# New orders around a dense tile, and one product of each tile moved from VectorE to ScalarE and GpSimd

## What is computed

```
q, k = rope(bf16(x @ Wq.T)), rope(bf16(x @ Wk.T))            # one head of 256
o    = sum over k <= q of exp(q.k / 16)                      # one number per row
x1   = layernorm(x + relu(o @ fc1_w.T + fc1_b) @ fc2_w.T + fc2_b)

xa   = x1 @ P_w.T                                            # 64 columns
Ci   = softmax over the top 3 of xa @ Ui.T, i = 1, 2, 3      # weights over 12 experts
h    = gelu(sum_e C1[:, e] * (x1 @ W1[e].T))                 # first mixture
y    = sum_e C2[:, e] * (h @ W2[e].T) + C3 @ b2              # second mixture, bias
out  = layernorm(x1 + y)
```

## Time and profile before

| | |
|---|---|
| median of 3 runs | 302.46 us (302.26 to 304.33) |
| profiled execution, its own time | 302.41 us |
| its span, first to last instruction | 300.5 us |
| busy in the span | PE 268.8 us (89%), DVE 239.7 (80%), ACT 164.0 (55%), POOL 148.8 (50%) |
| mean granted TensorE clock | 0.979 of full speed |

### The profile page before, as it was taken

The page is one execution under the profiler, slowest core; times in us unless marked ns, Lnnn a source line. Parts: engine busy times, 40 slices in busy tenths (PEclk is TensorE's granted clock), DMA queues, the critical chain, the costliest instruction groups (busy, mean ns, idle before and its releaser), DMA issues.

```text
span 300.5 us, 6389 instructions
## 1 busy us (share of the span) xinstructions
PE 268.8 (89%) x2028; PEld 195.1 (65%) x2030; DVE 239.7 (80%) x696; ACT 164.0 (55%) x341; POOL 148.8 (50%) x317
## 2 busy tenths in 40 slices
PE   6997999999896947999989989999999999999980
PEld 4443445544354724897877877877778788788960
DVE  0377689789708986689999999999999989987871
ACT  1246846663771645056656656846837847446430
POOL 2200008999998964242571572482373372573421
PEclk9999999999999995799999999999999999999998
DMA  8998999970000000000010001001000101011011
GB/s 229 403 397 279 164 193 205 150 100 0 0 3 0 0 3 0 0 12 29 17 27 28 22 17 37 20 19 38 19 20 22 34 20 35 21 35 30 27 35 40
DMA packets 19483, 20.50 MB, mean 68 GB/s; under 512 B 1636, under 2 KB 18808, under 8 KB 18936
## 3 DMA queue, kind: packets, MB, share of 16 engines
q1 hardware_dynamic: 18456, 19.13, 26.9%
q10 hardware_dynamic: 992, 0.93, 1.1%
HBM read 15.83 MB, written 4.19 MB: 67 GB/s over the span
## 4 chain that ended last, share of the span: by engine, by line
PE 39%; DVE 27%; POOL 15%; issue 7%; SPq 4%; DMA 4%; ACT 2%; DVEq 0%; POOLq 0%
PE bank L942 31%; DVE early L1309 10%; POOL W L417 5%; DMA W<-in_w2T 4%; POOL wtmp L414 4%; POOL W L416 3%; PE bank L780 2%; DVE early L1366 2%; SPq L341 2%; PE bank L828 2%; DVE st L1361 2%; DVE top L1177 2%; DVE x1T L1167 1%; DVE zrest L1192 1%; DVE xturn L1085 1%
## 5 line engine op out<-in xcount | busy, mean ns | idle before, releaser
L942 PE MATMUL bank<-W,early 128*128 (+1 forms) x630 | 76.9, 279 | 5.4 <-DVE early L1366 5.4
L942 PE MATMUL bank<-W,x1T 128*128 (+1 forms) x630 | 75.0, 273 | 2.3 <-ACT early L684 1.2
L942 PEld LDWEIGHTS bank<-W,early 128*128 128x128 f16 x630 | 61.0, 100 | 17.8 <-DVE early L1366 7.1
L942 PEld LDWEIGHTS bank<-W,x1T 128*128 128x128 f16 x630 | 59.8, 98 | 13.2 <-issue 2.9
L1309 DVE SCALAR_TENSOR_TENSOR early<-bank,Csel,early 128x256 f32<-128x256 f32 x124 | 59.8, 482 | 7.8 <-PE bank L942 3.2
L780 PE MATMUL bank<-early,wqk 128*128 128x512 f32 x128 | 60.3, 602 | 3.4 <-ACT qk L568 2.2
L1085 DVE TENSOR_TENSOR xturn<-qk,turn 128x2048 bf16<-128x2048 bf16 x16 | 21.4, 1335 | 21.1 <-ACT qk L568 21.0
L525 POOL TENSOR_SCALAR ve<-mv 128x1 f32<-128x1 f32 x32 | 7.3, 229 | 61.6 <-DVE mv L1362 60.8
L780 PEld LDWEIGHTS bank<-early,wqk 128*128 128x128 f32 x128 | 22.3, 190 | 23.8 <-issue 20.8
L689 ACT ACTIVATE early<-early 128x256 f32<-128x256 f32 x32 | 13.3, 417 | 44.8 <-DVE early L1309 44.6
L568 ACT ACTIVATE qk<-bank 128x512 bf16<-128x512 f32 x32 | 18.9, 594 | 28.8 <-PE bank L780 28.6
(11 more groups left out here) (116 smaller groups left out, 434.1 us busy)
## 6 DMA issues: line engine op xcount, KB each, us to landing
early<-in_xT SPq DMA_DIRECT2D x16, 256.0 KB, 7.2
xs<-in_x SPq DMA_DIRECT2D x32, 128.0 KB, 7.5
out<-early SPq DMA_DIRECT2D x32, 128.0 KB
W<-in_w1T SPq DMA_DIRECT2D x1, 2048.0 KB, 11.8
W<-in_w2T SPq DMA_DIRECT2D x1, 2048.0 KB, 12.4
W<-in_w1T SPq DMA_DIRECT2D x1, 1024.0 KB, 7.2
W<-in_w2T SPq DMA_DIRECT2D x1, 1024.0 KB, 14.0
wqk<-in_wqkT ACTq DMA_DIRECT2D x1, 512.0 KB, 3.8
```

The costliest lines, as they stand in the source:

```text
L942: mm = pe.matmul(where[:, 0:DIM], lhs(hx, c), w, start=(k == 0), stop=(k == 5))
```

## The change

Four things are changed.

1. **Bound of the second mixture's weights.** `w_sum` works in six halves rather than three pieces, and all six stand in chunks 2 and 3 rather than 1 and 2. `w_bound` and `peak_transpose` stand later in chunk 3.
2. **Orders between the chunk loop and turn 4.** Turns 1 to 3 are no longer turns of the loop: each engine has a list of its own. Tile 0's transposition and six of its second products stand right behind the first mixture of tile 1, in the order of experts 4 to 11, then 0 to 3 (`dense_expert`). The statistics of group 3 (`norm_stats(3)`) stand at the end of VectorE's list, `normed(3, 0)` near the end of ScalarE's, and the last `w_piece` ahead of `norm_scale(2)`.
3. **Tiles 2 to 30 (`late`).** The second mixture's first product is scaled by ScalarE into a buffer `part` (`begin_second`), VectorE adds the two others onto x1, and GpSimd adds `part` last (`late_add`).
4. **The rows' statistics, scale and final rows of those tiles come one turn later**: `row_stats`, `row_scale` and `final` of tile i-3 in turn i. In the last turn both tile 30 and tile 31 have theirs.

```
+        def late(t):
+            return 2 <= t < NT - 1
...
-                act = key[1] == 0 and key[2] == 0
+                act = key[2] == 0 and (key[1] == 0 or late(key[0]))
...
+        def dense_expert(m, j):
+            return (j + NB * m) % NE
...                                                        GpSimd
-            norm_scale(2)
             w_piece(piece)
+            norm_scale(2)
+            def late_add(t):
+                pool.wait_ge(acc_begun, taker[slot[t, 1, 0]][1])
+                pool.wait_ge(slot_added, by_dve[last(t, 1)])
+                pool.tensor_tensor(y[:, t % 4, :], y[:, t % 4, :], part[:, t % 2, :], ALU.add).then_inc(late_added, 1)
+            bias_add(0, 0)
+            bias_add(0, 1)
+            row_scale(0)
+            chosen_exps(1)
+            weights_of(1)
+            C3_split(1)
+            select_of(1)
+            row_scale(1)
+            norm_scale(3)
+            for i in range(GT, NT + 2):
                 aux(k, s, 0)
+                if late(i - 2):
+                    late_add(i - 2)
+                if late(i - 3):
+                    row_scale(i - 3)
+                if not late(i - 2):
+                    row_scale(i - 2)
                 aux(k, s, 1)
...                                                        ScalarE
-                act.activation(junk[:, :, :], Wf[:, WS:2 * WS, :][:, PARTS[q], :], ACT.Abs,
+                act.activation(junk[:, 2 * r:2 * r + 2, :], Wf[:, WS:2 * WS, :][:, HALVES[q], :], ACT.Abs,
...
+            def begin_second(t):
+                n = slot[t, 1, 0]
+                wait(act, late_added, t - 3)
+                act.wait_ge(slot_done, n + 1)
+                act.activation(part[:, t % 2, :], bank[place[n]][:, 0:DIM], ACT.Copy, scale=Csel[:, t, 1, 0:1])\
+                    .then_inc(acc_begun, 1)
...
+            h_high(2)
+            C3T_copy(1)
+            begin(3)
+            gelu(3)
+            normed(3, 0)
+            final(1)
+            for i in range(GT, NT + 2):
                 aux(k, s, 0)
+                if late(i - 2):
+                    begin_second(i - 2)
                 if i <= NT:
+                    h_high(i - 1)
                 aux(k, s, 1)
+                if i < NT:
                     begin(i)
                     gelu(i)
+                if late(i - 3):
+                    final(i - 3)
+                if not late(i - 2):
+                    final(i - 2)
...                                                        TensorE
             C3_transpose(0)
+            pe.wait_ge(exp_done, SPC * NCH)
+            h_transpose(0)
+            bias(0, 0)
+            routed_first(1)
+            route_logits(1)
+            pe.wait_ge(w_split, NM * (NE - NB) - 2)
+            second(0, range(0, 6))
             gate_transpose(NCH - 1)
+            bias(0, 1)
+            x1_transpose(2, 0)
+            pe.wait_ge(w_split, NM * (NE - NB))
+            second(0, range(6, NE - NB))
+            pe.wait_ge(wlo_done, NM * NB)
+            second(0, range(NE - NB, NE))
             pe.wait_ge(hgT_copied, NCH)
+            h_transpose(1)
+            routed_first(2)
+            route_count(1)
+            x1_transpose(2, 1)
+            fc(3, 0)
+            second(1, range(TOPK))
+            h_transpose(2)
+            fc(3, 1)
+            C3_transpose(1)
+            routed_first(3)
...                                                        VectorE
+            first_mixture(0, range(8, NE))
             norm_stats(2)
+            h_low(0)
+            first_mixture(1)
+            second_mixture(0, range(0, 3))
             w_low(NB + 2)
+            route_max(1)
+            second_mixture(0, range(3, 6))
             w_low(NB + 3)
+            second_mixture(0, (6, 7))
+            route_strike(1)
+            second_mixture(0, range(8, NE))
+            row_stats(0)
+            h_low(1)
+            x1_low(2, 0)
+            route_mask(1)
+            first_mixture(2)
+            route_sums(1)
+            fc_add(3, 0)
+            route_ids(1)
+            second_mixture(1)
+            row_stats(1)
+            x1_low(2, 1)
+            h_low(2)
+            fc_add(3, 1)
+            first_mixture(3)
+            norm_stats(3)
+            for i in range(GT, NT + 2):
                 aux(k, s, 0)
+                second_mixture(i - 2)
+                if late(i - 3):
+                    row_stats(i - 3)
+                if not late(i - 2):
+                    row_stats(i - 2)
+                if i <= NT:
+                    h_low(i - 1)
                 aux(k, s, 1)
+                if i < NT:
                     first_mixture(i)
```

More of the change, by code:

```diff
@@ L322, in build @@
         PARTS = (slice(0, NB), slice(NB + 2, NB + 6), slice(NB + 6, WS))
+        HALVES = [slice(p.start + 2 * n, p.start + 2 * n + 2) for p in PARTS for n in range(2)]
         block = ctx.enter_context(nc.Block())
@@ L692, in _ @@
                 qk_copy(c, 0)
+                if c == 3:
+                    w_sum(4)
                 qk_copy(c, 1)
@@ L711, in _, with h_high, final @@
                 early_aux(c, 3, early)
-                if c in (1, 2):
-                    w_sum(2 * (c - 1))
+                if c == 2:
+                    w_sum(2)
+                    w_sum(3)
                 if c in (4, 5):
                     w_high(2 * (c - 4) + 1)
+            def h_high(t):
+                act.wait_ge(hT_done, t + 1)
+                act.activation(hT[:, t % 2, 0, :, :].rearrange("p c n -> p (c n)"), bank[HT][:, 0:DIM], ACT.Copy,
+                               scale=ipow2[:, 1:2]).then_inc(hhi_done, 1)
+            def begin_second(t):
[4 more added lines that the diff above has]
+                    .then_inc(acc_begun, 1)
+            def final(t):
+                p = t % 2
+                act.wait_ge(rstd2_done, t + 1)
+                act.activation(y[:, t % 4, :], y[:, t % 4, :], ACT.Identity, bias=shift2[:, p:p + 1],
+                               scale=rstd2[:, p:p + 1]).then_inc(y_done, 1)
             x1_high(1, 1)
@@ L1011, in _, with h_transpose @@
             first(range(8, NE))
-            C3_transpose(0)
-            gate_transpose(NCH - 1)
-            aux(0, 0, 0)
-            load_ids(0)
-            mixture(1, 0, lambda hx, c: x1T[:, 1, hx, c, :], range(TOPK))
-            aux(0, 0, 1)
-            pe.wait_ge(exp_done, SPC * NCH)
-            pe.wait_ge(hgT_copied, NCH)
-            for i in range(1, NT + 2):
+            def h_transpose(t):
+                pe.wait_ge(gelu_done, t + 1)
+                wait(pe, hlo_done, t)
+                for c in range(NC):
+                    tr = pe.transpose(bank[HT][:, c * P:(c + 1) * P], hact[:, t % 2, c * P:(c + 1) * P], identf[:, :])
+                tr.then_inc(hT_done, 1)
@@ L1031, in _ @@
-                if i <= NT:
-                    t = i - 1
-                    pe.wait_ge(gelu_done, t + 1)
-                    wait(pe, hlo_done, t)
-                    for c in range(NC):
-                        tr = pe.transpose(bank[HT][:, c * P:(c + 1) * P], hact[:, t % 2, c * P:(c + 1) * P], identf[:, :])
-                    tr.then_inc(hT_done, 1)
-                aux(k, s, 1)
-                if 1 < i < NT:
-                    t = i
-                    if t % GT == 0:
-                        load_ids(t // GT)
-                    mixture(t, 0, lambda hx, c: x1T[:, t, hx, c, :], range(experts_of(t)))
+                second(i - 2, range(TOPK))
@@ L1323, in first_mixture, with second_mixture, row_stats, h_low @@
                     add_slot(t, 0, j, sums, sums)
+            def second_mixture(t, js=range(TOPK)):
+                sums = y[:, t % 4, :]
+                for j in js:
+                    if j == 0 and late(t):
+                        continue
+                    if j == (1 if late(t) else 0):
+                        dve.wait_ge(bias_added, t // 2 + 1)
+                        wait(dve, stored[t % 4], 16 * (t // 4))
+                        add_slot(t, 1, j, sums, xs[:, t, :])
+                    else:
+                        dve.wait_ge(slot_added, by_dve[t, 1, j] - 1)
+                        add_slot(t, 1, j, sums, sums)
+            def row_stats(t):
+                p = t % 2
+                dve.wait_ge(slot_added, by_dve[last(t, 1)])
+                if late(t):
+                    dve.wait_ge(late_added, t - 1)
+                wait(dve, rstd2_done, t - 1)
+                link(dve.bn_stats(st2[:, p, :], y[:, t % 4, :]))
+                dve.bn_aggr(mv2[:, p, :], st2[:, p, :]).then_inc(mv2_done, 1)
+            def h_low(t):
+                dve.wait_ge(hhi_done, t + 1)
+                dve.scalar_tensor_tensor(hT[:, t % 2, 1, :, :].rearrange("p c n -> p (c n)"), bank[HT][:, 0:DIM],
+                                         ipow2[:, 1:2], hT[:, t % 2, 0, :, :].rearrange("p c n -> p (c n)"),
+                                         ALU.mult, ALU.subtract).then_inc(hlo_done, 1)
             route_ids(0)
```

138 lines of the change are left out of this document (61 added, 77 removed).

## The result

The changed kernel takes 305.69 us (median of 20 runs, 303.47 to 308.64), the kernel before 302.28 (20 runs, 300.57 to 304.46): a ratio of 1.0096, 95% interval 1.0073 to 1.0119. The ratio is taken over the executions of both kernels, not from the two medians, whose quotient is 1.0113, and it leaves out the changed kernel's longest execution, which counts as slow. I had forecast 303.2 us, "within 1%" as the likeliest class, and 297.0 to 306.5 as the range; the median is inside it, 2.5 us above the point, and 0.2 us outside the case's own range of 300.5 to 305.5. The profiled execution took 304.10 us (span 302.3), 1.6 us less than the median.

What follows compares the result with a forecast made beforehand. VectorE and TensorE were taken as both near their bound in steady groups, with GpSimd nearly on the path; -0.6 - 0.8 + 2.5 - 1.6 + 1.25 = +0.75 on 302.41 gave 303.2 us, range 297.0 to 306.5.

Steps and rivals of the forecast that it cites:

- the case: The forecast itself: 303.2 us for the whole kernel, own range 300.5 to 305.5, chance 0.46.
- Step 3: Groups 1 to 4: GpSimd's late adds delay `bias_add` and `normed`, TensorE stops; 4 x 0.62 = +2.5 us.
- Step 4: Groups 5 to 7: no `normed` behind `bias_add`, so TensorE's waits for VectorE's low half go; -1.6 us.
- Step 1: Weights' bound in the chunk loop: the 2.22 us stall goes, a 1.7 us wait replaces 0.89; -0.6 us.
- Step 2: Dense stretch before turn 4: routing 1.8 us earlier, but `begin(4)` hardly moves; -0.8 us.
- Step 5: The end: tile 30's statistics and row steps stand ahead of tile 31's, delaying the last final row; +1.25 us.
- A: Rival: VectorE's relief pays in every one of groups 1 to 4, -1.1 us each; 296.3 us, chance 0.25.
- B: Rival: the dense stretch pays in full, 300.5 us, or 299 if TensorE keeps the high clock; chance 0.11.
- C: Rival: GpSimd's late adds and VectorE block each other in groups' turns 1 and 2; 307.8 us, chance 0.15.

Runs made afterwards that it cites:

- run 3: The changed kernel with `begin_second` ahead of `normed` on ScalarE in each group's fourth turn: 303.71 us, ratio 1.0032 to the kernel before.
- run 9: run 3 with GpSimd's second bias addition moved into its idle gap in the group's second turn: 302.55 us, ratio 0.9985 to the kernel before.
- run 12: run 10 with ScalarE's `normed(k + 3, 0)` moved into its gap between begin and gelu of the fourth turn: 291.39 us, ratio 0.9627.
- run 8: The changed kernel with run 7's orders, run 5's, new orders entering the groups, row scaling ahead of the late add, tile 30 not handed over: 298.76 us, ratio 0.9837.
- run 6: The changed kernel with GpSimd's `bias_add(k, 1)` at the start of the group's third turn, ahead of late add and row steps: 311.32 us, ratio 1.0263.
- run 7: The changed kernel with the orders of run 3 and run 6 together: 307.18 us, ratio 1.0118 to the kernel before.
- run 5: The changed kernel with VectorE's `w_bound` ahead of the first query rotation in the fourth chunk: 305.63 us, ratio 1.0066 to the kernel before.
- run 2: The kernel before with the hand-over of tiles 2 to 30 and later row statistics alone, without the new orders: 305.44 us, ratio 1.0095.
- run 10: run 8 with the bias addition in GpSimd's second-turn gap and the third turn's `norm_scale` behind its late add: 296.79 us, ratio 0.9798.
- run 11: The changed kernel with no tile handed over, run 5's order and new orders entering the groups: 299.55 us, ratio 0.9889 to the kernel before.

## Why the prediction was right, and where it was not

**Step 3, groups 1 to 4: right in mechanism, slightly large in size.** I had written `normed` later by 0.65 to 0.75, TensorE stopped "some 2 us" and periods of 24.0. Measured from the group's first route step, `normed` starts 0.68 later (20.25 us behind it, where it was 19.57); TensorE stops 1.92, and the periods are 23.85, 0.47 longer in place of 0.62. One sign did not come as written: `normed` waits for `bias_add` in four places, but 0.7 us and not over 1. The late add that no row had shown took 721 to 730 ns, where I had taken 0.7. One wait I had not seen: `final` for the row steps, 1.15 us, which stands ahead of the other. And one gain I had not counted: VectorE's cast in `route_ids` took 0.93 us in these groups before, and 0.19 us after, since `bias_add` no longer runs beside it (see step 4). Runs 3, 9 and 12 show the cycle by taking it apart, link by link. One stated bound was wrong: I called a period of 22.2 us the most that a faster VectorE can give. Run 12 reaches 21.8, all but 0.1 us of it TensorE's own work.

**Step 4, groups 5 to 7: the step that failed.** I wrote "There is no `normed` behind `bias_add` any more, so the relief counts", and -1.6 us. Measured: +0.35 in group 5, -0.74 in groups 6 and 7, -0.4 together. TensorE's waits for the low half in the steady turns did go, 1.6 us; in their place it waits 1.4 us for `begin_second`, in two places, and 0.57 for VectorE's L1264. The first, in the changed kernel:

```profile
242.08 0.72 POOL L535 TENSOR_TENSOR early<-early 128x256 f32<-128x256 f32 x1
...
243.86 0.27 POOL L543 TENSOR_SCALAR shift<-mv,rstd 128x1 f32<-128x1 f32 x1
...
244.16 0.60 ACT L775 ACTIVATE early<-early,shift,rstd 128x256 f32<-128x256 f32 x1 [1.20 <-POOL shift L543]
...
244.66 0.45 ACT L769 ACTIVATE early<-bank,Csel 128x256 f32<-128x256 f32 x1
...
245.17 1.49 PE L1018 MATMUL bank<-W,x1T 128*128 x12 [0.63 <-ACT early L769]
```

I had asked who stands behind `normed`, and not who stands behind `final`, though the change put a 0.7 us add ahead of the row steps for which `final` waits, and put a new instruction behind `final`. Run 8 turned the two around on GpSimd, among other edits; this stop is gone there, and group 5 went to 19.77.

The second is a collision that I had not looked for. VectorE's cast of 8 numbers in `route_ids` (L1314) ends 0.02 to 0.03 us after `bias_add` whenever it starts beside it, in all fourteen profiles:

```profile
247.38 1.27 POOL L447 TENSOR_TENSOR xs<-early,x 128x512 f32<-128x512 f32 x1
...
247.75 0.93 DVE L1314 CAST ids<-idf 1x8 int32<-1x8 f32 x1
248.60 0.67 DVE L1264 TENSOR_TENSOR x1T<-bank,x1T 128x512 f16<-128x512 f32 x1
...
249.41 0.39 PE L954 MATMUL bank<-cb,C 128*72 128x128 bf16 x4 [0.57 <-DVE x1T L1264]
```

It took 0.93 us here, 0.51 in the kernel before, and 0.18 in runs 6 and 7, where `bias_add` is done by then: there TensorE's 0.57 us are gone and group 5 takes 20.24, with the first stop still in place. So the later `bias_add` does cost in group 5, though no `normed` stands behind it.

**Step 1, the weights' bound: the wait was foreseen, its price was not.** Forecast: a wait of 1.7 us and -0.6 us net. Measured in the profile: 2.02 us, since x landed at 37.8 where I had 37.1, and -0.2. I treated a stop of TensorE as costing its own length. Of the seven traces with this stop, six have the clock down behind it, and the second route step 1.5 to 4 us later. That this is most of the median's excess over the profile is inferred from those profiles and the executions' mean clocks. Run 5, which took the stop away, recovered only 0.3%, with overlapping intervals; another stop and another stretch at 0.50 had come at 77 us.

**Step 2, the dense stretch: the total about right, by two errors that cancel.** Turn 4's route step came 3.4 us earlier (I had 1.8), `begin(4)` at 140.49 in place of 142.0. But TensorE idled 1.55 and 0.95 us there, and its granted clock was 0.54 in the next 3 us; with the hand-over's own 0.5 the first period took 3.2 us. The stretch at 0.50 that the kernel before had from 113.5 to 123.8 us is gone. At turn 8 the sum is -0.2; by steps 1, 2 and one group of step 3 I had -0.8.

**Step 5, the end: right.** +1.25 forecast, +1.19 measured, and gone when tile 30 was not handed over.

**The sum.** -0.2 at turn 8, which has a group's cost in it, then 1.4 for three more groups, 0.35, -0.74 and 1.19: +2.0 at the last row's start, and +1.69 in the profiled times, where I had +0.75. At the last row's start that is 1.27 too much: 0.6 from the time up to turn 8, -0.45 from three groups that cost less than forecast, 1.2 from step 4. The other 1.6 us between the point and the median are in no term of the sum: it was made for one profiled execution. That the median still lies in the range, by 0.8 us, and the ratio within 1%, by 0.04%, is in part luck.

**Rivals.** A fell because the relief is spent in the cycle; run 12 shows that it was there to be had, with periods below A's 22.3. B got its early turn 4 and lost it at once. C's price did not come: no late add took over 0.73 us, VectorE's adds kept to 0.42 to 0.49, and the mask instruction (L1301) took 0.75 us at the median and 1.30 at most, where it had a median of 1.11. But that GpSimd and VectorE hold each other up is seen, in the mask and in the cast of step 4; it was the old `bias_add` that did it, at its new times, and not the late add. For an addition of two inputs the Trainium skill, in "GPSIMD Engine Reference", section "Engine selection", says that GpSimd is about two times slower; here 725 ns against VectorE's 483 ns for 256 columns is 1.5, with one of VectorE's operands in PSUM.

## What to carry to other kernels

Here taking work off a busy engine paid only when the engine that received it had its idle time in the right place. Before handing work over, write down the receiver's run of instructions without a gap, and follow every engine that waits for an instruction behind the new one, not only the wait already visible. Here nearly the same work (tile 30 is not handed over) with all repairs, each a move within an engine's list and two of them into an existing gap, took 4.6% less time than as first ordered (ratios of 0.9627 and 1.0096). And when a median lies above its own profile, look for a place where other profiles of nearly the same kernel show a lower granted clock.

## What the runs showed that I had not expected

- A stop of TensorE has two prices. Behind 2.02 us at 40.6 the clock stayed at 1.00 in one profile; behind 2.08 to 2.83 us at the same place it fell to 0.50 for 3.4 to 6.8 us in six others. Behind the 2.0 and 2.2 us stop at 29 us, in the kernel before and in run 2, it did not fall at 39 to 48 us.
- Removing one stop moved it. With the maximum moved (runs 5, 8, 10, 11, 12) TensorE stops for 2.18 us at 76.5 to 77.1 for ScalarE's `normed`, and its granted clock is 0.50 for 3.4 us between 76.4 and 82.6 in each. The other nine profiles have no stop over 1.2 us from 71 to 80 us, and no low clock there. No run took that stop away, so what the second half of the gain is worth stays open.
- A VectorE instruction of 8 numbers took 0.16 to 0.20 us alone (from turn 4 on) and up to 1.08 us beside one GpSimd addition, and moving that addition was worth 0.6 us in group 5 (20.82 to 20.24).
- Placement outweighed amount: one GpSimd addition of 1.27 us per group cost nothing in one place and made the periods 0.8 us longer in another.
